# The end of a one-core adaLN attention block with a quantised gated feed-forward: one feed-forward product issued ahead of one gated product, and three engines' orders to match

## The reference

```
x  = x + gate1 * (attention(ln(x) * (1 + scale1) + shift1) @ out_w + out_b)
x2 = ln(x) * (1 + scale2) + shift2
x  = x + gate2 * (gelu(x2 @ ffn_w1 + b1) @ ffn_w2 + b2)          # the feed-forward (ffn1, ffn2)

def linear_bit(x, w, g):
    y = g * x * rsqrt(mean(x * x) + eps)                           # needs the squares of x
    s = 127 / max|y|                                               # needs the maximum of x * g
    return round(y * s) / s @ ternary(w)
h   = silu(linear_bit(x, w1, g1)) * linear_bit(x, w2, g2)          # the gated product
out = x_in + linear_bit(h, w3, g3)
```

## Time and profile before

| | |
|---|---|
| median of three runs | 338.66 us |
| the profiled execution, its own time | 338.6 us |
| its span, first to last instruction | 336.8 us |
| TensorE busy | 329.8 us, 98% |
| VectorE / ScalarE / GpSimd busy | 213.8 / 182.8 / 122.0 us |
| TensorE's granted clock, mean | 1.000 |

### The profile page before, as it was taken

The page is one execution under the profiler, slowest core; times in us unless marked ns, Lnnn a source line. Parts: engine busy times, 40 slices in busy tenths (PEclk is TensorE's granted clock), DMA queues, the critical chain, the costliest instruction groups (busy, mean ns, idle before and its releaser), DMA issues.

```text
span 336.8 us, 9812 instructions
## 1 busy us (share of the span) xinstructions
PE 329.8 (98%) x4195; PEld 298.8 (89%) x4195; DVE 213.8 (63%) x418; ACT 182.8 (54%) x354; POOL 122.0 (36%) x111
## 2 busy tenths in 40 slices
PE   8999999999999999999999999999999999999986
PEld 8889989899998989899898999889998889998765
DVE  3656966815859953505167236679565789886896
ACT  2754654454426365356423816478535576638794
POOL 2373505000934762555311413032620123304591
PEclk9999999999999999999999999999999999999999
DMA  7984930500055541210010000100020200200011
GB/s 231 374 291 167 304 129 2 159 1 2 2 147 168 159 157 34 64 33 2 2 55 12 3 20 13 47 19 3 2 62 2 64 3 2 64 1 2 0 33 62
DMA packets 20834, 24.41 MB, mean 72 GB/s; under 512 B 1780, under 2 KB 18328, under 8 KB 20792
## 3 DMA queue, kind: packets, MB, share of 16 engines
q1 hardware_dynamic: 20416, 23.50, 21.9%
q10 hardware_dynamic: 376, 0.30, 0.3%
HBM read 22.68 MB, written 1.11 MB: 71 GB/s over the span
## 4 chain that ended last, share of the span: by engine, by line
PE 93%; ACT 4%; DVE 2%; issue 1%; POOL 0%; ACTq 0%; DVEq 0%
PE proj_banks L564 40%; PE out_bank L564 16%; PE att_banks L657 8%; PE wide_banks L564 5%; PE turn_bank L564 3%; PE proj_banks L627 3%; PE wide_banks L848 3%; PE att_banks L892 2%; PE att_banks L564 2%; PE wide_banks L657 1%; ACT work L1858 1%; PE att_banks L848 1%; PE wide_banks L731 1%; PE proj_banks L848 1%; ACT L1717 1%
## 5 line engine op out<-in xcount | busy, mean ns | idle before, releaser
L1724 ACT ACTIVATE q_t<-proj_banks,bias_cols 128x256 f32<-128x256 f32 x64 | 30.5, 477 | 54.1 <-PE proj_banks L564 54.1
L564 PE MATMUL proj_banks<-x_hi,w_hi 128*128 128x256 f32 x252 | 52.8, 291 | 0.0
L564 PE MATMUL proj_banks<-x_lo,w_hi 128*128 128x256 f32 x252 | 50.7, 283 | 0.0
L564 PE MATMUL proj_banks<-x_hi,w_lo 128*128 128x256 f32 x252 | 50.7, 283 | 0.0
L1231 DVE TENSOR_TENSOR v_sb<-proj_banks,bv_row 128x512 f32<-128x512 f32 x32 | 21.8, 685 | 31.8 <-PE wide_banks L657 30.4
L564 PEld LDWEIGHTS proj_banks<-x_hi,w_hi 128*128 128x128 f32 x252 | 39.5, 191 | 1.5 <-issue 0.4
L564 PEld LDWEIGHTS proj_banks<-x_hi,w_lo 128*128 128x128 f32 x252 | 39.2, 191 | 0.0
L564 PEld LDWEIGHTS proj_banks<-x_lo,w_hi 128*128 128x128 f32 x252 | 39.1, 191 | 0.0
L657 PEld LDWEIGHTS att_banks<-probs_t,v_sb 32*128 32x128 f32 x512 | 29.8, 186 | 5.5 <-issue 5.4
L657 PE MATMUL att_banks<-probs_t,v_sb 32*128 32x32 f32 x512 | 31.6, 272 | 0.0
L1724 ACT ACTIVATE k_t<-proj_banks,bias_cols 128x256 f32<-128x256 f32 x64 | 30.2, 471 | 0.0
(11 more groups left out here) (324 smaller groups left out, 773.9 us busy)
## 6 DMA issues: line engine op xcount, KB each, us to landing
stage<-in_L_cond_qkv_w SPq DMA_DIRECT2D x16, 256.0 KB, 4.5
gate<-gate_rows_scratch SPq DMA_DIRECT2D x48, 64.0 KB, 2.5
stage<-in_L_cond_qkv_w SPq DMA_DIRECT2D x4, 512.0 KB, 5.4
stage<-in_L_cond_out_w SPq DMA_DIRECT2D x4, 512.0 KB, 4.5
work<-in_L_ffn_w SPq DMA_DIRECT2D x2, 1024.0 KB, 9.9
xin<-in_x SPq DMA_DIRECT2D x7, 256.0 KB, 2.9
bv_row<-in_L_cond_qkv_b SPq DMA_DIRECT2D x4, 256.0 KB, 5.4
work<-in_L_cond_ada_w SPq DMA_DIRECT2D x1, 1024.0 KB, 9.3
```

The lines of the kernel that those rows point to most:

```text
L564: mm = pe.matmul(dst, l, r, start=start and i == 0, stop=stop and i == len(seq) - 1)
L1724: act.activation(dst[:, h, :], proj_bank[h % 2][:, s * QT:(s + 1) * QT], ACT.Identity, bias=bias_cols[:, c:c + 1]).then_inc(qk_kept, 1)
```

## The change

On TensorE z(1) moves from in front of `end_ffn2(b, 2)` and `end_ffn2(b, 3)` to behind them. VectorE's h(1) moves behind `last_gate` and `last_add`. Further on VectorE the product for the dequantising factor moves ahead of the rounding, `scale_of` and `inverse_of` change places with neighbours, and `round_last(0)` moves behind the last maximum. ScalarE takes silu(0) ahead of `keep_q(a, 1)`, and the squares of the very last tile ahead of `late_round(0)`. GpSimd makes the inverse roots ahead of weighing 1, and weighs half 5 ahead of `hidden_rms(a, 1)`. No instruction is added or taken away; SyncE's order is the same.

```diff
@@ TensorE
             end_z(0)
-            end_z(1)
             end_ffn2(b, 2)
             end_ffn2(b, 3)
+            end_z(1)
             end_z(2)
@@ VectorE
             end_hidden(0, late_h)
-            end_hidden(1, late_h)
             last_gate(b)
             last_add(b)
+            end_hidden(1, late_h)
             weighed = last_weigh(b)
             maxima = last_amax(weighed)
             inverse = last_inverse(maxima)
             last_scale(b, inverse)
+            product = last_product(b)
             last_round(b)
-            product = last_product(b)
             last_deq(b, product)
             end_hidden(2, late_h)
             end_hidden(3, late_h)
             dve.wait_ge(h_weighted, 2)
             maximum0 = hidden_max(a, 0, late_hw[0])
             inverse0 = inverse_of(a, 0, maximum0)
-            scale_of(a, 0, inverse0)
             end_hidden(4, h_tiles)
             end_hidden(5, h_tiles)
             dve.wait_ge(h_weighted, 4)
             maximum1 = hidden_max(a, 1, late_hw[1])
+            scale_of(a, 0, inverse0)
             end_hidden(6, h_tiles)
+            inverse1 = inverse_of(a, 1, maximum1)
             end_hidden(7, h_tiles)
-            inverse1 = inverse_of(a, 1, maximum1)
-            scale_of(a, 1, inverse1)
             dve.wait_ge(h_ready, 4 * b + 4)
             weighed = weigh(h_tiles[1][:, half[1]], g3_row[:, half[1]], late_weighted[:, 1, half[1]])
             dve.wait_ge(h_weighted, 6)
             last_maximum0 = hidden_max(b, 0, late_weighted[:, 0, :])
+            scale_of(a, 1, inverse1)
             last_inverse0 = inverse_of(b, 0, last_maximum0)
             scale_last(0, last_inverse0)
-            round_last(0)
             dve.wait_ge(h_weighted, 7)
             ffn_after(weighed)
             last_maximum1 = hidden_max(b, 1, late_weighted[:, 1, :])
+            round_last(0)
@@ ScalarE
             load_table(ACT.Silu)
+            end_silu(0)
             keep_q(a, 1, wide_bank[1])
-            end_silu(0)
             end_silu(1)
@@
             square_hidden(b, 0, None, 8)
+            square_hidden(b, 1, None, 8)
             late_round(0)
-            square_hidden(b, 1, None, 8)
             late_round(1)
@@ GpSimd
             end_weigh(0, late_hw[0], late_h[0])
-            end_weigh(1, late_hw[0], late_h[0])
             rms_of_both(b)
             hidden_rms(a, 0)
+            end_weigh(1, late_hw[0], late_h[0])
@@
             end_weigh(4, late_weighted[:, 0], h_tiles[0])
+            end_weigh(5, late_weighted[:, 0], h_tiles[0])
             hidden_rms(a, 1)
-            end_weigh(5, late_weighted[:, 0], h_tiles[0])
```

## The result

The changed kernel took 341.41 us, median of five runs (340.17 to 341.63), beside 338.55 for the kernel before in the same session (338.37 to 338.77). The ratio is 1.007, 95% interval 1.006 to 1.0081. So it is slower, by 0.6 to 0.8%. The median stands 0.4 above the range's upper end of 341.0 and 1.2 above the forecast.

What follows compares the result with a forecast made beforehand. The prediction took a chain of waits across the engines in the last 29 us as the bound. Span 336.8 + 1.54 for ScalarE's later copy gave 338.3, time 340.1; with 0.1 for VectorE's end, 340.2 us, range 339.2 to 341.0.

Steps and rivals of the forecast that it cites:

- the mechanism: Moving z(1) makes silu(1), h(1) and ScalarE's squares late, so GpSimd's root decides VectorE's scale; chance 0.64.
- main term: On VectorE, quarter b's scale starts 1.31 us later, waiting for GpSimd's root behind ScalarE's late squares; bounds 1.2 to 1.45.
- TensorE's first gap: TensorE idle about 1.4 us behind its filler, before quarter b's transposes at about 319.25.
- product ahead of the rounding: VectorE's small 128x4 product after the scale hides behind the scale's handover: cost 0.00, at most 0.1 us.
- VectorE is neutral: With h(1) in front, VectorE's weighing starts at 314.24 against 314.23; the 0.86 us won go on waiting for silu(1).
- later moves: VectorE's scale_of adds 0.13 us before h(6), inverse_of 0.12 before h(7); ScalarE's last squares go ahead of both roundings.
- VectorE's end: VectorE's last weighing, maximum and round_last(0) meet TensorE with margins of 0.1 to 0.3 us: 0.1 given, upper bound 0.7.
- rival E: TensorE's longer idle times bring back the half-speed clock, doubling products from 329.4 to 334.1: up to +4.6 us; chance 0.06.
- rival D: GpSimd's and VectorE's last weighings, maxima and round_last run past TensorE's new places by 0.3 to 0.7 us; chance 0.16.

Runs made afterwards that it cites:

- both gaps filled: The changed kernel with keep_running(8) made 12 and the third keep_running(4) made 12, adding unread matmuls in TensorE's two idle times: 340.53 us.
- the one with the late squares back: The changed kernel with late_round(0) again ahead of ScalarE's squares of the last tile: 340.59 us.
- all three mended: The changed kernel with quarter b's squares first, weighing 1 held behind the dequantising factor, late_round(0) again ahead of the last tile's squares: 339.11 us.
- my own: The kernel before, with ScalarE's squares of quarter a's second tile ahead of silu(4), VectorE's maximum behind h(7), last weighing on GpSimd, L2221 last: 339.03 us.

## Why the prediction was right, and where it was not

**Right: the mechanism and its main term.** With the trace's shift of 0.17: silu(1) forecast 312.77, found 312.61; h(1) 313.57, found 313.41; the weighing unchanged, found so; quarter `b`'s squares read out 317.06, found 316.91; the root's end 318.30, found 318.14; the scale 318.34, found 318.17. TensorE's first gap was 1.27, forecast about 1.4. The run with the squares moved put the scale back to 316.95, and z(1) moved with the product ahead of the rounding measured the term alone: 1.2 us, forecast 1.31.

**Right: VectorE is neutral, the later moves cost a few tenths.** ScalarE's copy came 1.41 later (1.58 with the shift), forecast 1.54. The later moves alone cost 0.1 to 0.3 at full clock. VectorE's last weighing took 0.75, not 1.42: GpSimd's weighing 5 ended 0.2 behind its start (326.51, and 326.31), before 0.87 behind it (326.18, and 325.31).

**Right in sum at full clock.** 340.17 and 340.71 in the two such runs, forecast 340.2. With both gaps filled the profile has 1.58 more than before, forecast 1.54 and 0.1 for VectorE's end; the medians of this kernel and of the one with the late squares back, 340.53 and 340.59, are 0.3 to 0.4 higher, and in the profiles of these two the filler starts 0.45 and 0.46 later than before, which is no part of the change.

**Wrong: rival E, by chance and by price.** This is the step that took the median above the range: in the sum the clock stood at nothing, and it cost 1.4 in the profiled run. I gave it a chance of 0.06 with the words "No idle time this long stands in the old tail". That was a statement on the old kernel, and says nothing of what a longer gap does. I had worked out the gap (about 2.2, found 2.10), but not asked what a longer gap than the old 0.87 would do. The clock fell in three runs of five. Over all kernels here with this gap at about 2.1 it fell in 23 of 40 runs (3 of 5, 4 of 6, 2 of 5, 7 of 12, 7 of 12). In those with only the first gap, of 1.27, it fell in 3 of 21; in those with neither (both filled, all three mended, my own) in 0 of 27, and in the kernel before in 0 of 55. The price that I gave, up to 4.6, took it that the clock stays low to the end; it came back after 3.4 us in each of the six profiles in which it fell. It cost 1.4 in the change's profile and 1.7 behind the first gap. Between runs of one kernel the difference goes up to 2.3; where in the tail it fell in the unprofiled ones is not known.

**Wrong in part: rival D.** In the change weighings and maxima were in time; in the kernel with all three mended `round_last(0)` is about 0.2 late. But collisions of VectorE and GpSimd matter here more than I had it: three of my own edits ran into one that the change's order happens to avoid. It was luck for the forecast that the change avoids them; the prediction did not look for them there. The product ahead of the rounding, which I priced at a cost of 0.00 to 0.1, gains 1.07 (340.91 against 339.84; 0.90 between the profiles) once z(1) is moved. In the sum of the change it does not show, because there both stand together.

The sum from the profiles, each counted from its filler's start to VectorE's last output:

| kernel | us | more than before |
|---|---|---|
| before | 18.14 | |
| z(1) moved, product ahead of the rounding | 19.53 | 1.39 |
| the change with both gaps filled | 19.72 | 1.58 |
| the change, clock fallen | 21.12 | 2.98 |
| all three mended | 18.39 | 0.25 |

So the 2.9 us between the medians are: 1.2 (runs) to 1.4 (rows) for the late squares, about 0.2 for the later moves on top of them, and 1.4 for the clock in the runs that lose it.

## What to carry to other kernels

When a move makes one result late, go through every in-order queue in which somebody waits for it, and ask what stands behind the waiting instruction: here VectorE lost nothing and ScalarE's queue carried the whole delay to a reader three engines away. When a move lengthens an idle time of TensorE, price the clock with it, and time more than one run: the loss comes in some runs only and hides in a median. Before you free GpSimd or shift its work, lay its instructions beside VectorE's; with two engines that exclude each other, an instruction that is in time can cost more than a late one.

## What I had not expected of the hardware

The granted clock fell behind a gap of 2.1 us (0.51 from 330 to 332 us) and in one profile behind one of 1.27 us (0.50 from 322 to 324), both between stretches in which TensorE worked, and not in every run of the same kernel; in the kernels whose longest gap there was 0.87 us or less (the one before, the one with both gaps filled, the one with all three mended, my own) it read 0.999 or 1.000 in every run. An operation of VectorE on 128x4 elements took 1.18 us instead of 0.16 beside a weighing of GpSimd, two roundings 1.68 instead of 0.62; and the other way round GpSimd's first step of the root, on two numbers a partition, took 0.87 instead of 0.19 beside VectorE's weighing L1399.
